# Gated feed-forward stages of a four-layer macaron network: the order of the down products, of the residual additions and of the layer norm that follows them

## The reference, cut to what matters

```
x = x + 0.5 * ffn1(layernorm(x))      # twice, before and after the attention of layer 1

def ffn1(x):
    shared = (silu(x @ ws_gate.T) * (x @ ws_up.T)) @ ws_down.T          # 128 inner features
    scores = sigmoid(x @ gate_weight.T)                                 # 8 experts
    w, idx = top_k(scores, 2);  w = 2.5 * w / (w.sum() + 1e-20)
    routed = sum over the two experts e of  w_e * (silu(x @ w_gate[e].T) * (x @ w_up[e].T)) @ w_down[e].T   # 64 inner features each
    return routed + shared
```

## Time and profile before

| | |
|---|---|
| median of three runs | 1514.79 us (1512.69 to 1522.83) |
| profiled execution, its time | 1510.44 us |
| its span, first to last instruction | 1508.6 us |
| TensorE busy | 1200.5 us, 80% of the span |
| VectorE, ScalarE, GpSimd busy | 877.3, 636.2, 554.9 us |
| block ffn1_0 | 445.0 to 528.2 us of the span |
| block ffn1_1 | 798.4 to 883.4 us of the span |

### The profile page before, as it was taken

One profiled execution on the slowest core, in us unless ns is written; L12 is line 12 of the kernel. 1 busy time (PEld: TensorE's weight loads), 2 busy tenths in 40 slices (PEclk: granted clock), 3 DMA queues, 4 the chain that ended last, 5 costly groups with the idle time before them and its releaser, 6 DMA issues. The chain is left out here.

```text
span 1508.6 us, 30132 instructions
## 1 busy us (share of the span) xinstructions
PE 1200.5 (80%) x11545; PEld 690.5 (46%) x11553; DVE 877.3 (58%) x2261; ACT 636.2 (42%) x1318; POOL 554.9 (37%) x652
## 2 busy tenths in 40 slices
PE   3995788886969658999988886674995888898598
PEld 2563344444655425555544542432673222333277
DVE  5047667731154468787735567794147988893215
ACT  1221555641322135666543133240333576776143
POOL 5753123113410078898320000136463231222342
PEclk9996999997979879999998988695996699999699
DMA  6533422104710047665509000003342221210344
GB/s 133 148 98 98 92 85 78 43 10 121 216 43 1 0 122 213 180 189 155 152 28 123 18 8 0 1 16 91 110 131 74 73 76 44 61 33 16 85 131 115
DMA packets 140600, 128.64 MB, mean 85 GB/s; under 512 B 19101, under 2 KB 123945, under 8 KB 140464
## 3 DMA queue, kind: packets, MB, share of 16 engines
q1 hardware_dynamic: 128640, 104.64, 26.3%
q0 software_dynamic: 9184, 20.81, 4.0%
q10 hardware_dynamic: 2640, 1.36, 0.7%
HBM read 79.80 MB, written 47.69 MB: 85 GB/s over the span
## 5 line engine op out<-in xcount | busy, mean ns | idle before, releaser
L2471 DVE TENSOR_REDUCE att_maxima<-psum 128x2 f32<-128x1024 f32 (+3 forms) x384 | 354.3, 949 | 110.4 <-PE psum L2115 47.4
L2350 ACT ACTIVATE att_probs<-psum 128x512 f32<-128x512 f32 (+1 forms) x640 | 322.4, 556 | 190.7 <-PE psum L2111 74.5
L108 POOL TENSOR_TENSOR rstd<-var_eps,neg_half 128x4 f32<-128x4 f32 x44 | 45.1, 1026 | 461.0 <-DVE var_eps L99 461.0
L2094 PE MATMUL psum<-att_queries,att_keys 50*32 50x384 bf16 (+4 forms) x1280 | 156.1, 328 | 35.6 <-ACT att_probs L2350 18.6
L2100 PE MATMUL psum<-att_keys,att_queries 48*32 48x384 bf16 (+4 forms) x1280 | 154.1, 345 | 11.7 <-DVE att_maxima L2471 11.7
L1045 POOL DMA_INDIRECT returned<-moe_out,moe_slot_tokens x101 | 101.7, 1007 | 118.3 <-DVE moe_out L973 92.0
L839 ACT ACTIVATE moe_hidden<-psum,moe_b 128x320 f32<-128x320 f32 (+1 forms) x128 | 77.8, 608 | 127.4 <-PE psum L752 126.9
L172 PE MATMUL psum<-ident,normalised_rows 128*128 128x128 f32 x192 | 43.3, 367 | 99.3 <-DVE normalised_rows L117 78.4
L2094 PEld LDWEIGHTS psum<-att_queries,att_keys 50*32 50x32 bf16 (+1 forms) x1280 | 45.6, 92 | 153.9 <-issue 74.1
L759 PE MATMUL psum<-moe_w,moe_hidden 128*128 128x128 f32 (+1 forms) x784 | 109.5, 286 | 0.0
L752 PE MATMUL psum<-moe_slot_columns,moe_w 128*128 128x320 f32 (+1 forms) x256 | 98.2, 527 | 2.9 <-ACT moe_slot_columns L834 2.9
(11 more groups left out here) (297 smaller groups left out, 2358.1 us busy)
## 6 DMA issues: line engine op xcount, KB each, us to landing
moe_w<-l_w SPq DMA_DIRECT2D x64, 256.0 KB, 3.2
score_terms<-att_parts SPq DMA_DIRECT2D x32, 384.0 KB, 2.9
moe_back<-returned SPq DMA_DIRECT2D x24, 256.0 KB, 4.3
att_queries<-score_terms SPq DMA_DIRECT2D x64, 96.0 KB
att_keys<-score_terms SPq DMA_DIRECT2D x64, 96.0 KB
att_queries<-score_terms SPq DMA_DIRECT2D x16, 384.0 KB, 4.3
att_keys<-score_terms SPq DMA_DIRECT2D x16, 384.0 KB, 5.6
score_terms<-att_parts POOLq DMA_DIRECT2D x12, 384.0 KB, 3.2
```

Of the source, the lines that this page charges most:

```text
L2094: col = nc.tensor.matmul(g.psum[one, cols_bank + h, c0:c0 + w], k_op[own_rows, ci, p, key], q_op[own_rows, ci, p, first_query[s]:T], start ...
L2350: nc.scalar.activation(probs[:, G % 2, 2 * p + r, unit_at[u]:unit_at[u] + w], g.psum[:, cols_bank + r, 0:w], ACT.Exp).then_inc(probs_ready, 1)
L2471: ins = nc.vector.tensor_reduce(maxima[:, G % 2, t, 2 * p:2 * p + 2], g.psum[:, rows_bank(k):rows_bank(k) + 2, c0:c0 + w], axis=AX, op=ALU ...
```

## The change

In `ffn1`, `down(b)` becomes `down(b, c)`: the four products of one chunk, one for each row tile. `start` is set only for the first product of a batch; the other three row tiles have their first product without it. A batch's chunks 0 and 1 are multiplied in unit (b, 2), chunk 2 in (b, 3), chunk 3 in (b, 4) and chunk 4 in (b+1, 0). The addition of batch b-1 goes behind unit (b, 0) of VectorE's list, its statistics behind (b, 1), its rows behind (b, 2); its turn goes to (b, 3) on TensorE, its columns to (b, 4) on ScalarE, its logits to (b, 4) on TensorE and their copy to (b+1, 1) on ScalarE. Behind the last unit remain only chunk 4 of batch 3 and what follows it for batch 3.

```diff
@@ -1126,15 +1126,15 @@
 
         @block.tensor
         def _(pe):
-            def down(b):
-                pe.wait_ge(hidden, chunks * (b + 1))
-                if b >= 1:
+            def down(b, c):
+                pe.wait_ge(hidden, chunks * b + c + 1)
+                if c == 0 and b >= 1:
                     pe.wait_ge(summed, b)
                 for i in range(GROUP):
-                    for c in range(chunks):
-                        mm = nc.tensor.matmul(y_bank[:, i * D:(i + 1) * D], hid[:, b % 2, c, i * P:(i + 1) * P],
-                                              wd_sb[:, c, :], start=(c == 0), stop=(c == chunks - 1))
-                mm.then_inc(y_psum, 1)
+                    mm = nc.tensor.matmul(y_bank[:, i * D:(i + 1) * D], hid[:, b % 2, c, i * P:(i + 1) * P], wd_sb[:, c, :],
+                                          start=(c == 0 and i == 0), stop=(c == chunks - 1), skip_group_check=True)
+                if c == chunks - 1:
+                    mm.then_inc(y_psum, 1)
 
             def gate_up(k):
                 b, c = units[k]
@@ -1168,15 +1168,20 @@
                         pe.wait_ge(hidden, k)
                     nc.tensor.matmul(cb_bank[:], g.expert_selector[:, c, :], combine_t[:, b * T:(b + 1) * T],
                                      start=True, stop=True).then_inc(cb_psum, 1)
-                if c == 1 and b >= 1:
-                    down(b - 1)
-                if c == 0 and b >= 2:
-                    ln_transpose(g, pe, ln, b - 2, xnt_bank, one_bank=True)
-                if c == 2 and b >= 2:
-                    ln_logits(g, pe, ln, b - 2, xnt_bank)
-            ln_transpose(g, pe, ln, B - 2, xnt_bank, one_bank=True)
-            down(B - 1)
-            ln_logits(g, pe, ln, B - 2, xnt_bank)
+                if c == 0 and b >= 1:
+                    down(b - 1, 4)
+                if c == 2:
+                    down(b, 0)
+                    down(b, 1)
+                if c == 3:
+                    down(b, 2)
+                    if b >= 1:
+                        ln_transpose(g, pe, ln, b - 1, xnt_bank, one_bank=True)
+                if c == 4:
+                    down(b, 3)
+                    if b >= 1:
+                        ln_logits(g, pe, ln, b - 1, xnt_bank)
+            down(B - 1, 4)
             ln_transpose(g, pe, ln, B - 1, xnt_bank, one_bank=True)
             ln_logits(g, pe, ln, B - 1, xnt_bank)
 
@@ -1197,11 +1202,10 @@
                 if k == 1:
                     copy_combine(0)
                     copy_combine(1)
+                if c == 4 and b >= 1:
+                    ln_columns(g, act, ln, b - 1, xnt_bank)
                 if c == 1 and b >= 2:
-                    ln_columns(g, act, ln, b - 2, xnt_bank)
-                if c == 3 and b >= 2:
                     ln_copy_logits(g, act, ln, b - 2, xnt_bank)
-            ln_columns(g, act, ln, B - 2, xnt_bank)
             ln_copy_logits(g, act, ln, B - 2, xnt_bank)
             ln_columns(g, act, ln, B - 1, xnt_bank)
             ln_copy_logits(g, act, ln, B - 1, xnt_bank)
@@ -1259,11 +1263,11 @@
                 else:
                     nc.vector.tensor_tensor(dst, silu[:, k % 2, :], u_bank[k % 2][:], ALU.mult).then_inc(hidden, 1)
                     nc.vector.memset(g.spare[:], 0.0).then_inc(gated, 1)
+                if c == 0 and b >= 1:
+                    add(b - 1)
+                if c == 1 and b >= 1:
+                    ln_stats(g, v, ln, b - 1)
                 if c == 2 and b >= 1:
-                    add(b - 1)
-                if c == 3 and b >= 1:
-                    ln_stats(g, v, ln, b - 1)
-                if c == 4 and b >= 1:
                     ln_rows(g, v, ln, b - 1)
             add(B - 1)
             ln_stats(g, v, ln, B - 1)
```

## The result

The changed kernel took 1495.42 us (median of four runs, 1487.46 to 1499.11), the kernel before 1515.82 (four runs, 1512.69 to 1522.83). The ratio is 0.9875, with a 95% interval of 0.9841 to 0.9909: faster by 1.25%, 20 us where 19.5 were forecast.

A forecast was written before the change was run, and what follows sets the result against it. TensorE was taken as the bound, with waits within batches and a pause and half clock at block ends. Gains of 10.8 and 8.7 us, 19.5 in all, from the 1514.79 us median gave 1495.3 us; range 1488 to 1505.

The forecast's parts named there:

- What bounds the kernel: In both ffn1 blocks TensorE is busiest; its work in ffn1_0 is 14.35 us of a 15.95 us batch period.
- The waits within the batches: TensorE's waits between the first down and last combine product, 3.20 us in ffn1_0 and 3.25 in ffn1_1, go to zero.
- The narrowest place: Gate product of (b,3), needing VectorE's multiplication of (b,1) behind the addition: 0.11 us of slack left.
- The switches: 24 more switches between kinds of TensorE products cost nothing; at most one exposed instruction each, 2.7 us.
- The ends: At each block's end the last addition starts sooner, by 10.8 us in ffn1_0 and 8.7 us in ffn1_1.
- the 0 to 0.5 allowed: Last turn of each block at half clock behind its pause: between 0 and 0.5 us lost per block.
- 2 us of clock: Next block's first products may run at either clock level; loss taken as 0, with 2 us to both sides.
- The rule of the Trainium skill: Idle TensorE drops to half clock until busy again; so the last turn runs at half clock in both kernels.
- The waits did not stay: Rival: all present waits within batches remain, 6.45 us missing, gain 13.1, 1501.7 us; chance 0.15.
- given back downstream: Rival: attention of layer 1 and later stages lose 6 us or more of the gain, 1501 us or more; chance 0.07.
- The slower rival: Each stretch of down chunks costs TensorE a restart, decisive from 0.81 us a switch; 1531 us at 1.5; chance 0.03.

The follow-up runs named there:

- Experiment 1: Kernel before with only the block's end changed: batch 3's down product chunk by chunk, last chunk ahead of batch 2's turn; ratio 0.9916 to before.
- experiment 3: Changed kernel with addition, statistics, rows, turn, columns and logits of a batch one unit later each; ratio 0.9906 to the kernel before.
- experiment 4: Changed kernel with four of five down chunks per batch cut in two, 16 more switches between kinds of products per block; ratio 0.9938 to before.
- experiment 5: Changed kernel with an unread fill of about 0.5 us on VectorE behind each addition of batches 0 to 2; ratio 0.9893 to before.
- experiment 6: Kernel before with 16 unread bf16 products in TensorE's pause ahead of batch 2's turn at each block's end; ratio 0.9947 to before.
- experiment 7: Changed kernel with 20 unread bf16 products behind the last down chunk and 3 behind the turn; ratios 0.9873 and 0.9854 to before.

## Why the prediction was right, point by point

*What bounds the kernel.* Right. TensorE without a wait sets the period: 14.35 us forecast, 14.35 measured; in ffn1_1 15.2 forecast, and the additions of batches 1 and 2 are 15.24 apart.

*The waits within the batches* were put at 6.45 us of the gain, all of it to go. Experiment 1 keeps them and is 4.8 us behind the changed kernel. That isn't 6.45, because experiment 1 also has the turn and the logits of batch 2 behind the last chunk, off the path to the last addition: 6.45 - 2 x 0.44 - 0.81 = 4.76. This is worked out, no run separates it. The direct measure is the period, 1.60 us less in ffn1_0. The 0.42 us by which experiment 3 is shorter in ffn1_1 may be of the same kind: its logits of batch 2 stand behind the last chunk.

*The narrowest place.* Forecast slack 0.11 us. In the trace after the multiplication ends at 468.75 + 0.69 = 469.44 and the gate product starts at 469.76; with the 0.15 of the earlier trace rows the slack is 0.17, and experiments 4 and 5 took it away: 0.5 us more on VectorE costs 0.38 a batch, and TensorE 0.4 us sooner at this place 0.13. The addition came 1.09 us after the start of its down chunk (466.93 to 468.02), where 0.89 + 0.27 were assumed.

*The switches* were taken at nothing with a far end of 2.7 us. That holds: the period of the changed kernel has no room for them (14.35 us, the bare work), and in experiment 4 the rows keep their pace across 32 more.

*The ends.* Forecast: last addition sooner by 10.8 and 8.7 us. Measured from the second combine product: 62.76 to 51.79 is 10.97 in ffn1_0, 63.09 to 54.53 is 8.56 in ffn1_1. What follows the addition grew by 0.26 us in ffn1_0, since the last turn ran wholly at half clock (1.11 us), within the 0 to 0.5 allowed. Experiments 1 and 6 split it: 14.5 us come from the ends alone, of which 4.5 were the clock; the other 10 are the two pauses (4.8 and 4.7 us) and half a microsecond that no run separates. The block ffn1_0 is 70.83 us long and not 72.4, because the clock rose sooner at its start, which the prediction left to its 2 us of clock; ffn1_1 is 76.37 where 76.6 were said.

*The rule of the Trainium skill* (TensorE: Matmul & The Clock Gate, part 1: an idle TensorE is put back to half its clock until it is busy again). The rows agree: 0.50 behind the pause in the kernel before, and with products in the pause 1.00 (experiments 6 and 7).

*The rivals.* The waits did not stay. Whether something was given back downstream no single profile can show, since the attention alone varies by more; but the changed kernel's three ratios to the one before (0.9875, 0.9869, 0.9870) are 19 to 20 us, as much as its blocks gained. With 6 us given back the gain would be 13.5, below what two of the three intervals allow (13.8 and 15.8 us at the least). The slower rival needed 0.81 us a switch, and the rows show none.

*The total* of 1495.3 us met 1495.42 partly by luck: the profile had 23.0 us of difference, 19.3 by the change and 3.5 by the clock at the start of ffn1_0 and by stages that the change doesn't touch.

## What to carry to other kernels

Sum the work of the busiest engine over one period, compare it with the period, and read the difference as what an order of issue can give; then walk the new order once, and write down the smallest slack, because that is what the next change will break. A product that waits whole for the last of its inputs both starves the other engines and leaves itself for the end of the stage; cut into pieces and issued as inputs come, the cuts themselves cost nothing here. Where they stand does count: pieces moved ahead of a narrow place brought TensorE there sooner and cost 0.13 us a batch (experiment 4). At a block's end look at the clock as well: a pause of 4.8 us cost its own length and 2.85 us more in the products behind it (experiment 6, ffn1_0).

## What the runs showed of the hardware

- The same start of a block, with the same instructions, took from 12.15 to 14.83 us up to the second combine product, by when the granted clock rose; two profiles can differ by 2.7 us in one stage with the same code. The granted clock over it was 0.82 in the shortest (ffn1_1 of the changed kernel) and 0.62 in the longest (ffn1_1 of experiment 3).
- Products that nobody reads, bf16 128x512 at 0.21 us each, kept the granted clock at 1.00 through a pause of 4.7 us, and three more over the barrier into the next stage, whose first product comes 0.62 us after the last of them (experiment 7: eight products in 3.67 us and not 6.29).
- A switch between f32 products of 128x512 and a stretch of four instructions of 128x128 costs nothing that a row shows: 0.86, 0.44 and 0.86 us from start to start, as without it (experiment 4).
- The attention stage, the same program in twelve profiles, took 267.2 to 281.7 us. A change of a few us in one stage of this kernel can't be read from the length of another.
